# Two norms from one set of moments, and one of five difference passes moved from GpSimd to VectorE

## The reference

```
s1, s2 = q k1^T * SCALE, q k2^T * SCALE            (causal)
attn = softmax(s1) - sigmoid(lambda_logit) * softmax(s2)
attn = attn / max(sum(|attn|), 1e-6)
x = layernorm(x + (attn v) Wo^T)                    (eps 1e-5)
xn = (x - mean) * rsqrt(var + 1e-5) * gamma + beta  (the router's and experts' input)
probs = softmax(xn router_w^T / 1.5);  w, idx = top 2
out = sum of w * (silu(xn W1) W2) over the two experts
x = layernorm(x + out + x)
```

## Time and profile before

| what | us |
|---|---|
| median of 3 runs (lowest, highest) | 1209.85 (1205.65, 1212.59) |
| the profiled execution | 1201.04 |
| its span, first to last instruction | 1199.3 |
| POOL busy | 948.1 |
| PE busy | 927.8 |
| DVE busy | 924.3 |
| ACT busy | 851.7 |

### The profile page before, as it was taken

The page is one execution under the profiler, slowest core; times in us unless marked ns, Lnnn a source line. Parts: engine busy times, 40 slices in busy tenths (PEclk is TensorE's granted clock), DMA queues, the critical chain, the costliest instruction groups (busy, mean ns, idle before and its releaser), DMA issues.

```text
span 1199.3 us, 27952 instructions
## 1 busy us (share of the span) xinstructions
PE 927.8 (77%) x8522; PEld 738.7 (62%) x8522; DVE 924.3 (77%) x2393; ACT 851.7 (71%) x2706; POOL 948.1 (79%) x1257
## 2 busy tenths in 40 slices
PE   2588787868898788967799688977799787959582
PEld 1355564647676567846677466756578576748582
DVE  1588898859997799968997799968997689946242
ACT  1598987669887777868787777878788777853140
POOL 3399999898878997899878998799878898793402
PEclk9577788669998898989898898979998788978797
DMA  3703400533246524382235623382244632245662
GB/s 115 156 1 91 104 2 14 136 110 109 78 125 161 159 69 128 111 234 71 85 106 144 192 72 118 99 236 73 85 125 125 182 92 79 81 130 172 214 194 72
DMA packets 117046, 139.39 MB, mean 116 GB/s; under 512 B 11042, under 2 KB 99490, under 8 KB 116898
## 3 DMA queue, kind: packets, MB, share of 16 engines
q1 hardware_dynamic: 112802, 129.21, 37.4%
q0 software_dynamic: 4096, 8.40, 2.4%
HBM read 107.81 MB, written 29.75 MB: 115 GB/s over the span
## 4 chain that ended last, share of the span: by engine, by line
POOL 34%; DVE 22%; PE 19%; issue 12%; ACT 6%; DMA 5%; SPq 2%; DVEq 0%; POOLq 0%; ACTq 0%
POOL exps L614 13%; POOL exps L610 11%; DVE neg_max L962 7%; POOL x_sorted_dram L630 4%; PE trans L1124 4%; ACT exps L680 4%; POOL y_back L639 3%; DVE abs_sum L972 3%; PE scores L1090 3%; PE side L1067 3%; PE side L1073 3%; POOL lam_l L604 1%; DVE stats L760 1%; DMA xg<-x_sorted_dram 1%; DVE hT L924 1%
## 5 line engine op out<-in xcount | busy, mean ns | idle before, releaser
L680 ACT ACTIVATE exps<-scores,neg_max 128x512 f32<-128x512 f32 (+3 forms) x1024 | 539.2, 541 | 74.8 <-DVE neg_max L962 72.7
L962 DVE TENSOR_REDUCE neg_max<-scores 128x1 f32<-128x512 f32 (+3 forms) x896 | 424.6, 526 | 79.4 <-PE scores L1092 75.1
L614 POOL TENSOR_TENSOR exps<-exps 128x512 f32<-128x512 f32 x320 | 406.5, 1270 | 26.7
L610 POOL TENSOR_SCALAR exps<-exps,inv_l,lam_l 128x512 f32<-128x512 f32 (+3 forms) x512 | 312.4, 616 | 59.1 <-DVE inv_l L953 42.1
L1124 PE MATMUL trans<-ident,exps 128*128 128x128 f32 x1280 | 242.6, 320 | 148.4 <-POOL exps L614 114.0
L1124 PEld LDWEIGHTS trans<-ident,exps 128*128 128x128 f32 x1280 | 161.4, 160 | 216.3 <-POOL exps L614 169.6
L1090 PE MATMUL scores<-stack 72*128 72x512 bf16 (+3 forms) x1024 | 279.9, 343 | 15.5 <-DMA stack<-parts_dram 14.9
L972 DVE TENSOR_REDUCE abs_sum<-exps 128x1 f32<-128x512 f32 (+3 forms) x448 | 224.6, 525 | 67.6 <-POOL exps L614 67.2
L687 ACT ACTIVATE diffT<-trans 128x512 f32<-128x512 f32 x320 | 194.4, 608 | 95.2 <-PE trans L1124 93.8
L680 ACT ACTIVATION_READ_ACCUMULATOR exps<-scores,neg_max 128x1 f32 x1024 | 226.1, 221 | 0.0
L1092 PE MATMUL scores<-causal_bf,ident_bf 128*128 128x128 bf16 x1024 | 215.4, 243 | 0.0
(11 more groups left out here) (142 smaller groups left out, 871.9 us busy)
## 6 DMA issues: line engine op xcount, KB each, us to landing
w_sb<-w_dram SPq DMA_DIRECT2D x120, 512.0 KB, 3.7
stack<-parts_dram SPq DMA_DIRECT2D x288, 96.0 KB
parts_dram<-parts SPq DMA_DIRECT2D x104, 128.0 KB, 2.4
xg<-x_sorted_dram SPq DMA_DIRECT2D x24, 256.0 KB, 3.6
y_sorted_dram<-y_sorted SPq DMA_DIRECT2D x24, 256.0 KB, 3.8
x_in<-x_dram SPq DMA_DIRECT2D x8, 256.0 KB, 4.6
x_res<-x_dram SPq DMA_DIRECT2D x8, 256.0 KB, 4.6
o_dram<-y_out SPq DMA_DIRECT2D x8, 256.0 KB, 2.2
```

Of the source, the lines that this page charges most:

```text
L610: nc.gpsimd.tensor_scalar(diff[:, ring, col:col + w], exps[:, ring, 1, col:col + w], inv_l2[:, i:i + 1], lam_l1[:, i:i + 1], ALU.mult, ALU ...
L614: nc.gpsimd.tensor_tensor(diff[:, ring, :], diff[:, ring, :], exps[:, ring, 0, :], ALU.subtract)\
L680: nc.scalar.activation(exps[:, ring, k, col:col + w], scores[:, c % 2, k, col:col + w], ACT.Exp, bias=neg_max[:, c % 2, k, i:i + 1], accum ...
L962: nc.vector.tensor_reduce(neg_max[:, c % 2, k, i:i + many], scores[:, c % 2, k, col:col + many * w].rearrange("p (i w) -> p i w", w=w), AX ...
```

## The change

1. The moments of r1 serve both norms. If v is the variance of r1, the first norm's factor is (v+eps)^-1/2, and the norm of its result has factor (v/(v+eps)+eps)^-1/2 on top; multiplied out, (v(1+eps)+eps^2)^-1/2. POOL makes both roots in one pow over 8 columns; the first with 0.25 inside the root, so that it gives twice x1 directly. `norm1` and `norm2` become one step, `norms`; x1 itself is no longer written.
2. Chunks of kind 0 get their difference from DVE at slot c+3: one small instruction multiplies the first exponential's sum, lambda and `inv_l2` to a column `coef`, and one pass computes exp2*coef-exp1 over 512 columns. POOL skips the chunk but for `lam_l1`, which kind 1 needs. Waits for a difference go by `diff_ready`.
3. `LAG_ABS` is 5 in place of 4.
4. Many slots of the tables move, by up to five.

```
-LAG_ABS = 4
+LAG_ABS = 5
+DVE_KINDS = (0,)
-POST_SLOTS = {... "divide": 10, "out_proj": 12, "norm1": 16, "norm2": 18, "xn_T": 21, "logits": 22, ..., "count": 30, ...}
+POST_SLOTS = {... "divide": 11, "out_proj": 12, "norms": 17, "xn_T": 21, "logits": 23, ..., "count": 29, ...}
-COMBINE_SLOTS = (86, 87, 88, 89, 90, 91, 92, 93)
+COMBINE_SLOTS = (86, 86, 88, 90, 90, 91, 92, 93)
-STACK_SLOT = 33
+STACK_SLOT = 31
...
+        def diff_ready(n, c):
+            pair, kind = divmod(c, KINDS)
+            here = kind in DVE_KINDS
+            same = [i for i in range(KINDS) if (i in DVE_KINDS) == here]
+            made, count = (diff_dve_done if here else diff_done), pair * len(same) + sum(i <= kind for i in same)
+            return made.sem, made.after(n, count)
...  (POOL)
+                        if kind in DVE_KINDS:
+                            continue
...
+                        if name == "out_proj":
+                            pool.wait_ge(moments_done.sem, moments_done.after(n, 1))
+                            nc.gpsimd.tensor_scalar(var_eps[:, 0, :], mv[:, 0, :, 1], EPS, 0.25, ALU.add, ALU.mult)\
+                                .then_inc(eps_added.sem, 1)
+                            nc.gpsimd.tensor_scalar(var_eps[:, 1, :], mv[:, 0, :, 1], 1.0 + EPS, EPS * EPS, ALU.mult, ALU.add)\
+                                .then_inc(eps_added.sem, 1)
+                            pool.wait_ge(eps_added.sem, eps_added.after(n, 2))
+                            nc.gpsimd.tensor_tensor(rstd[:, 0:2, :], var_eps[:, 0:2, :], minus_half[:, 0:2, :], ALU.pow)\
+                                .then_inc(rstd_done.sem, 1)
...  (DVE)
-                        if name == "norm1":
-                            normalise(n, 0, x1, r1).then_inc(x1_done.sem, 1)
-                            dve.wait_ge(x1_done.sem, x1_done.after(n, 1))
-                            moments(n, 1, x1)
-                        if name == "norm2":
-                            if n:
-                                dve.wait_ge(scattered.sem, scattered.after(n - 1, TOP * NT))
-                            nc.vector.tensor_scalar(x1_twice[:, n % 2, :, :], x1[:, :, :], 2.0, None, ALU.mult)\
-                                .then_inc(acc_set.sem, 1)
-                            normalise(n, 1, xh, x1).then_inc(xh_done.sem, 1)
+                        if name == "norms":
+                            dve.wait_ge(rstd_done.sem, rstd_done.after(n, 1))
+                            normalise(x1_twice[:, n % 2, :, :], r1, 0, 0).then_inc(acc_set.sem, 1)
+                            if n:
+                                dve.wait_ge(scattered.sem, scattered.after(n - 1, TOP * NT))
+                            normalise(xh[:, :, :], r1, 0, 1).then_inc(xh_done.sem, 1)
...
+                    for n, c in chunks(b, stages, slot, LAG_EXP + 2):
+                        pair, kind = divmod(c, KINDS)
+                        if kind in DVE_KINDS:
+                            (t, _, second, _, i), ring = next(units_of(c)), ring_e(n, c)
+                            h = head_of(pair, second)
+                            ...
+                            nc.vector.scalar_tensor_tensor(out=coef[:, i:i + 1], in0=sums[:, 0, i:i + 1],
+                                                           scalar=lam_all[:, h:h + 1], in1=inv_l2[:, i:i + 1],
+                                                           op0=ALU.mult, op1=ALU.mult).then_inc(coef_done.sem, 1)
+                            dve.wait_ge(coef_done.sem, coef_done.after(n, count))
+                            nc.vector.scalar_tensor_tensor(out=diff[:, ring, :], in0=exps[:, ring, 1, :],
+                                                           scalar=coef[:, i:i + 1], in1=exps[:, ring, 0, :],
+                                                           op0=ALU.mult, op1=ALU.subtract).then_inc(diff_dve_done.sem, 1)
```

More of the change, by code:

```diff
@@ L83 @@
 SIDE = {}
[L84 to L89, removed]
+POST_SLOTS = {"spread": 8, "den_T": 10, "divide": 11, "out_proj": 12, "norms": 17, "xn_T": 21, "logits": 23, "router_exp": 24, "count": 29, "place": 31, "sorted": 43, "norm3": 96, "finish": 98}
+HIDDEN_SLOTS = (45, 47, 49, 51, 53, 55, 59, 60, 64, 66, 68, 70, 72, 74, 76)
+EXPERT_SLOTS = (48, 50, 52, 54, 56, 58, 62, 63, 67, 69, 71, 73, 75, 76, 78)
+WEIGHT_SLOTS = (41, 43, 45, 47, 49, 51, 55, 56, 61, 62, 62, 66, 68, 69, 69)
+TURN_SLOTS = (44, 51, 58, 66)
+Y_OUT_SLOTS = (57, 67, 77, 83)
 SCATTER_SLOTS = (31, 32, 33, 34, 35, 36, 37, 38)
 GATHER_SLOTS = (82, 83, 85, 85, 86, 88, 89, 90)
-COMBINE_SLOTS = (86, 87, 88, 89, 90, 91, 92, 93)
-STACK_SLOT = 33
+COMBINE_SLOTS = (86, 86, 88, 90, 90, 91, 92, 93)
+STACK_SLOT = 31
 WEIGHTS_AHEAD = 4
@@ L641, in body @@
                                 bass.IndirectOffsetOnAxis(ap=place_int[:, n % 2, i:i + 1], axis=0)).then_inc(gathered[i].sem, 16)
[L642 to L653, removed]
+                        if name == "out_proj":
[7 more added lines that the diff above has]
+                                .then_inc(rstd_done.sem, 1)
+                        if name == "norm3":
+                            pool.wait_ge(last_moments.sem, last_moments.after(n, 1))
+                            nc.gpsimd.tensor_scalar(var_eps[:, 2, :], mv[:, 1, :, 1], EPS, None, ALU.add)\
+                                .then_inc(last_eps.sem, 1)
+                            pool.wait_ge(last_eps.sem, last_eps.after(n, 1))
+                            nc.gpsimd.tensor_tensor(rstd[:, 2, :], var_eps[:, 2, :], minus_half[:, 0, :], ALU.pow)\
+                                .then_inc(last_rstd.sem, 1)
             pool.wait_ge(lam_done, 2)
@@ L670, in body @@
                             if k == 0:
[L672 removed]
+                                act.wait_ge(*diff_ready(m, used))
                             else:
@@ L755, in _, with moments @@
                 nc.vector.memset(turn_no[:, j:j + 1, :], float(j))
-            def moments(n, i, src):
+            def moments(i, src):
                 for t in range(NT):
@@ L763, in moments, with normalise @@
                     last = nc.vector.bn_aggr(mv[:, i, t, :], stats[:, i, t, :])
-                last.then_inc((moments_done if i < 2 else last_moments).sem, 1)
-            def normalise(n, i, dst, src):
-                if i < 2:
-                    dve.wait_ge(rstd_done.sem, rstd_done.after(n, i + 1))
-                else:
-                    dve.wait_ge(last_rstd.sem, last_rstd.after(n, 1))
+                return last
+            def normalise(dst, src, i, scale):
                 for t in range(NT):
                     last = nc.vector.tensor_scalar(dst[:, t, :], src[:, t, :], mv[:, i, t, 0:1],
-                                                   rstd[:, i, t:t + 1], ALU.subtract, ALU.mult)
+                                                   rstd[:, scale, t:t + 1], ALU.subtract, ALU.mult)
                 return last
@@ L941, in body @@
                             dve.wait_ge(combined.sem, combined.after(n, TOP * NT))
-                            moments(n, 2, acc)
+                            moments(1, acc).then_inc(last_moments.sem, 1)
                         if name == "finish":
                             dve.wait_ge(y_stored.sem, y_stored.after(n - 1, 1))
-                            normalise(n, 2, y_out, acc).then_inc(y_done.sem, 1)
+                            dve.wait_ge(last_rstd.sem, last_rstd.after(n, 1))
+                            normalise(y_out, acc, 1, 2).then_inc(y_done.sem, 1)
                     for n, c in chunks(b, stages, slot, LAG_EXP + 1):
```

39 lines of the change are left out of this document (21 added, 18 removed).

## The result

The changed kernel takes 1170.10 us (median of 4 runs, 1165.71 to 1172.52); the kernel before beside it 1207.99 us. The ratio is 0.9694, 95% interval 0.9652 to 0.9735: 3.1% faster, where 1.6% was forecast. The sign was right, the change forecast (18 us) was half of what came (38 us), and the measured time lies in the stated range but outside the likeliest case's own (1180 to 1203).

The account below looks back on a forecast made before the run. Different limits by stage: POOL in scatters and gathers, DVE in norms and routing, PE in counting. Six bodies at -2.0 (-12), first two -4, tail -2.3 sum to -18 us: 1191 us, range 1158 to 1224.

Parts of the forecast that it names:

- relief of 2.2 us per chunk: POOL, kind-0 chunks: dropping L610 and L614 saves 2.2 us per chunk, 64 chunks in all.
- A: Scatter stage of the repeated body, 24 us: POOL stays the limit, -3.0 us per body.
- B: Gather stage of the repeated body, 34 us: the limit passes from POOL to DVE, -1.7 us per body.
- D: Counting and placing stage of the repeated body, 26 us: PE holds, change 0.
- low end of the price (0.9): DVE's coefficient and pass without POOL conflict: 0.9 us per chunk; high end 2.95, taken 1.6.
- What the pass costs POOL: DVE's pass holds POOL up in its turn, by about 0.3 us per chunk.
- LAG_ABS 5 and the slots: Later read of L972, post slots moved, stack loads issued two slots earlier: cost and gain nil.
- C term: Norms, parts and routing stage, 52 us, DVE busy 49.9: +4.8-1.6-0.5 = +2.7 us per body.
- rival 2: Scatter and gather stages' gain doesn't arrive, as what stands behind POOL comes at once: 1210 us, chance 0.19.
- 2.1 us for the norms: DVE, norms stage: 1.6 us of removed work and 0.5 us fewer conflicts per body.
- Rival 1: The DVE-POOL conflict hardly happens, price 0.9 us per chunk: -46 us, 1164 us, chance 0.24.
- The tail: Chain from L772 to xh, 2.8 us, less 0.5 for second epsilon and wider power: -2.3 us.

Follow-up runs that it names:

- old slots: Norms, pass and LAG_ABS 5 as in the changed kernel, with the slot tables of the kernel before: ratio 1.003 to the kernel before.
- new slots with POOL's pass: The changed kernel with the kind-0 difference back on POOL; merged norms, LAG_ABS 5 and moved slots stay: ratio 1.008 to the kernel before.
- without the relief: The changed kernel with POOL making all differences and DVE doing coefficient and pass over spare tiles: ratio 1.052, 1272.18 us.
- sorted, stack and experts: Norms, pass, LAG_ABS 5 in slots of before, adding in turn sorted rows at 43, stack loads from 31, five experts' tables as changed: 0.9966, 0.979, 0.974.
- one-input kernel: The changed kernel with DVE's coefficient and pass replaced by operations reading one SBUF operand, kind-0 difference not made: ratio 0.947 to the kernel before.
- last two experiments: The changed kernel with stack loads at 33, plus the y_out steps of before (0.971) or the combine steps of before (0.967).

## Why the prediction was off

**Right.** POOL bounds from scatter to r1. Its relief of 2.2 us per chunk came in full from scatter to gather, and from there to r1 the limit passed to DVE. A and B together: -4.7 forecast, -6.4+1.2 = -5.2 measured (-5.3 in the means), in part by luck: the measured stretch takes in half of D, for which nothing was forecast, and B grew where -1.7 was forecast. The low end of the price (0.9) and its derivation: the two medians with the same waits and overlap give 0.93. What the pass costs POOL (0.3 forecast, 0.44 measured). `LAG_ABS` is worth nothing.

**The step that failed** is "LAG_ABS 5 and the slots ... Cost and gain nil", for the slots, and with it the C term of the sum. I priced the pass on a fixed schedule and the slots on the kernel before, each alone, and there both are worth about nothing (0.8% and 0.3%). Together they are worth 4.2%. In the old slots, what stood behind POOL came at once: scatter to gather gained 3.4 us and gather to r1 lost 4.3. That it would not be so in the new slots I had not asked, though the change showed the sorted rows and the stack moved ahead. The time of that kernel, 1210.13, is that of rival 2 (1210), but this is luck: rival 2 had A keep its length, B shrink by 1.7 and C grow by 2.7, and the kernel before ran 5 us faster on that chip.

From r1 to the first scatter, the C term, the two causes can be told apart in the table above: the new slots with POOL's pass take 66.6 us and the changed kernel 66.4; old slots 68.5 without and 69.1 with the pass. So the slots give 2 to 2.7 us there, and the pass costs between nothing and 0.6 where I had put 4.8 for it. The price itself was nearly right: without the relief it costs 5.5 us there (66.6 to 72.1). What was wrong is that I counted nothing for POOL's relief in C ("relief of POOL pays in A and B, and DVE pays for it in C"): it gives the 5.5 back (72.1 to 66.4). And the 2.1 us for the norms did not come (68.6 to 68.5). Together C gave -2.2 where +2.7 was forecast, and these 5 us in each of six bodies are more than the whole gap of 20 us between forecast and result; the tail took some back.

**The price was over-sized as well.** Over the run DVE's busy time grows by 58 to 61 us through the pass (906.1 to 966.7 in old slots, 893.3 to 951.3 in new), 0.9 us per chunk net, not 1.6. The new instructions take 1.33 in the mean, 0.13 of it overlapped. The rest comes from DVE's other instructions: from the kernel with POOL's pass to the changed one they get shorter by 18.6 us in all, 2.3 per body, where I had counted 0.5 for conflicts. Most of that is in the first normalise (550 ns in the mean to 349) and the casts of the parts (718 to 572). Not all gain: the guard goes from 295 to 355, and one form of the combine from 440 to 530. So it fits a POOL with less to read, but where each step lands beside POOL counts too. Rival 1 had this price of 0.9 and nearly the time (1164), yet it did not come true: its reason was that the conflict hardly happens, and 54 of 64 chunks meet it; and in the old slots the same net price brings no gain at all.

The Trainium skill (SBUF — State Buffer, Who interferes with whom) says that the lock is exclusive and that the order of issue decides who blocks. The runs agree with the lock (pass 750 ns alone, up to 1069; 1055 in the mean beside a busier POOL) and show that POOL waits too: its own instructions get longer in turn. Its scale of 128x384 takes 732 ns in the mean in the changed kernel and 669 in the one with POOL's pass:

```profile
L623 POOL TENSOR_SCALAR exps<-exps,inv_l,lam_l 128x384 f32<-128x384 f32 x128 | 93.7, 732 | 28.3 <-DVE inv_l L963 24.5
```
```profile
L623 POOL TENSOR_SCALAR exps<-exps,inv_l,lam_l 128x384 f32<-128x384 f32 x128 | 85.6, 669 | 1.8
```

**The tail** was forecast at -2.3 us and lost about 10: from the last copy of the values to the end it takes 249.9 us, before 240.2. Whether the kernel or the chip is behind this is open (last section), so it isn't shown that the result would be near 4% without it.

**Which slot it is** stays partly open. Added to the old slots, sorted, stack and experts bring 0.7, 1.8 and 0.5%; taken from the new, 0.9, 0 and up to 0.9%. They seem to stand in for one another. What goes along with the time is DVE's wait for scores, 86.9 us in old slots, 81.2, 60.8, 57.7 along the additions and 50.4 in the changed kernel: 36.5 us where the time fell by 41. That these come from SP's queue, in which stack loads, weights and sorted rows stand in one row, is only shown for the sorted rows (22.7 us of PE's waits to 2.1, of which the stack's slot alone takes 10.9 to 1.7). The 2 us that the slots give from r1 to scatter belong to none of the tables alone: with the single steps, the experts' tables, the combine or the stack of before that stretch stays at 65.8 to 66.9.

## What to carry to other kernels

When a change relieves the bounding engine and moves its schedule too, price the relief twice: in the old schedule, and with what stands next moved out of the way. If a transfer is due at a fixed slot behind the work that gets shorter, it is the next wait. Relief of the busiest engine can also count in a stage where another is busier: here it gave back the whole price of the pass in C. And where two engines block each other, a move of work can cost less than the sum of the new instructions, since others on the receiving engine wait less (here 18.6 us of 85).

## What was not expected of the hardware

GpSimd's power goes largely by its columns: 8 took 1.68 us and 4 took 1.04 (duration min/median/max in the kernel with norms alone), so merging the two roots saves 0.4 of 2.1 us. In the changed kernel the 8 columns took 2.07 in the median, which is all of the two: there DVE's new pass stands beside them, and POOL pays for the conflict. In the tail, where no pass is, and in the one-input kernel they took 1.68. Norms alone, then the changed kernel, then its timeline at 171 us:

```profile
L662 POOL TENSOR_TENSOR rstd<-var_eps,minus_half x8: 1669/1677/1682, 180.3 to 1103.7; 128x8 f32<-128x8 f32 x8
...
L669 POOL TENSOR_TENSOR rstd<-var_eps,minus_half x8: 1030/1042/1052, 447.5 to 1208.1; 128x4 f32<-128x4 f32 x8
```
```profile
L662 POOL TENSOR_TENSOR rstd<-var_eps,minus_half x8: 1675/2066/2072, 172.1 to 1057.3; 128x8 f32<-128x8 f32 x8
...
L669 POOL TENSOR_TENSOR rstd<-var_eps,minus_half x8: 1028/1042/1153, 433.3 to 1162.8; 128x4 f32<-128x4 f32 x8
```
```profile
171.84 0.75 DVE L977 SCALAR_TENSOR_TENSOR exps<-exps,coef 128x512 f32<-128x512 f32 x1
172.08 2.04 POOL L662 TENSOR_TENSOR rstd<-var_eps,minus_half 128x8 f32<-128x8 f32 x1
```

In the tail PE stands between matmuls that wait for no semaphore. After (timeline of PE, start and us):

```profile
1035.74 1.16 PE L1139 MATMUL heads<-diffT,v_sb 128*32 128x128 f32 x31
1037.37 0.41 PE L1139 MATMUL heads<-diffT,v_sb 128*32 128x128 f32 x4 [0.47 <-issue]
1038.77 0.33 PE L1139 MATMUL heads<-diffT,v_sb 128*32 128x128 f32 x2 [0.98 <-issue]
1039.52 0.27 PE L1139 MATMUL heads<-diffT,v_sb 128*32 128x128 f32 x1 [0.42 <-issue]
1040.23 0.39 PE L1139 MATMUL heads<-diffT,v_sb 128*32 128x128 f32 x2 [0.45 <-issue]
```

The same place before:

```profile
1080.86 1.30 PE L1113 MATMUL heads<-diffT,v_sb 128*32 128x128 f32 x40
1082.09 1.16 PE L1067 MATMUL side<-xgT,w_sb 128*128 128x128 f32 x8
```

From the sixth gather group's first DMA to the last r1 it takes 13.1 us before, 22.8 after and 20.9 in the kernel with the norms alone, which explains most of that kernel's 1.1%. The gaps add up to 3.4 us after; the rest goes with the granted clock (0.78 in this stretch, 0.90 before). The stretch takes 19.7 us or more in every trace but three: the kernel before (13.1) and the last two experiments (14.7 and 14.3), which are the only two that ran on the chip where the kernel before takes 1193 us. Their ratios are no better than the others', which speaks for the chip rather than the kernel. What starves PE there was not tried.
